# Per-head products in a vision tower: full-height matmuls split into two row halves, in two phases

## What is computed

```
kv = jnp.einsum('bhlk,bhlv->bhkv', k, v)
out = jnp.einsum('bhlk,bhkv->bhlv', q, kv)
```

## Time and profile before

| | us |
|---|---|
| median of 3 runs | 1691.65 (1689.15 to 1692.24) |
| the profiled execution, its own time | 1688.76 |
| its span in the profile | 1686.6 |
| TensorE matmul busy | 1482.2 (88%) |
| TensorE weight loads busy | 1437.1 (85%) |
| VectorE busy | 1020.7 (61%) |
| ScalarE busy | 872.3 (52%) |
| GpSimd busy | 111.1 (7%) |

### The profile page before, as it was taken

One profiled execution on the slowest core, in us unless ns is written; L12 is line 12 of the kernel. 1 busy time (PEld: TensorE's weight loads), 2 busy tenths in 40 slices (PEclk: granted clock), 3 DMA queues, 4 the chain that ended last, 5 costly groups with the idle time before them and its releaser, 6 DMA issues. The chain is left out here.

```text
span 1686.6 us, 32100 instructions
## 1 busy us (share of the span) xinstructions
PE 1482.2 (88%) x9909; PEld 1437.1 (85%) x9909; DVE 1020.7 (61%) x2461; ACT 872.3 (52%) x3121; POOL 111.1 (7%) x240
## 2 busy tenths in 40 slices
PE   5899999999999999999999999999999998563211
PEld 5899999999999999999999999999999997441110
DVE  6765566666665655556555565556665542766676
ACT  4455555555555555555555555555555555541320
POOL 0000000000000000000000000000000000000000
PEclk9999999999999999999999999999999999556555
DMA  9211111111111111111111111111100001374007
GB/s 200 74 44 44 43 42 42 42 42 42 42 42 42 42 42 40 40 40 40 41 42 42 42 42 42 42 42 42 42 10 10 10 10 39 122 268 174 0 0 305
DMA packets 53092, 99.34 MB, mean 59 GB/s; under 512 B 16705, under 2 KB 35649, under 8 KB 52033
## 3 DMA queue, kind: packets, MB, share of 16 engines
q1 hardware_dynamic: 50768, 96.91, 19.7%
q10 hardware_dynamic: 2288, 2.00, 0.6%
HBM read 73.17 MB, written 25.69 MB: 59 GB/s over the span
## 5 line engine op out<-in xcount | busy, mean ns | idle before, releaser
L613 ACT ACTIVATE ffn<-ffn 128x196 f32<-128x196 f32 x1024 | 329.7, 322 | 236.8 <-PE ffn L504 236.3
L504 PE MATMUL ffn<-x_t_hi,pat_w_hi 128*128 128x392 f32 x1024 | 360.6, 352 | 1.7 <-DVE x_t_lo L772 1.7
L504 PE MATMUL ffn<-x_t_hi,pat_w_lo 128*128 128x392 f32 x1024 | 348.6, 340 | 0.0
L504 PE MATMUL ffn<-x_t_lo,pat_w_hi 128*128 128x392 f32 x1024 | 348.2, 340 | 0.0
L435 PE MATMUL gen<-qkvu_w_hi,h_t_hi 128*98 128x256 f32 x768 | 215.4, 280 | 1.4 <-ACT q_t L571 1.4
L435 PE MATMUL gen<-qkvu_w_hi,h_t_lo 128*98 128x256 f32 x768 | 215.0, 280 | 0.0
L435 PE MATMUL gen<-qkvu_w_lo,h_t_hi 128*98 128x256 f32 x768 | 214.7, 280 | 0.0
L504 PEld LDWEIGHTS ffn<-x_t_hi,pat_w_hi 128*128 128x128 f32 x1024 | 193.1, 189 | 2.0 <-DVE x_t_lo L772 2.0
L504 PEld LDWEIGHTS ffn<-x_t_lo,pat_w_hi 128*128 128x128 f32 x1024 | 194.3, 190 | 0.0
L613 ACT ACTIVATION_READ_ACCUMULATOR ffn<-ffn 128x1 f32 x1024 | 194.3, 190 | 0.0
L504 PEld LDWEIGHTS ffn<-x_t_hi,pat_w_lo 128*128 128x128 f32 x1024 | 192.9, 188 | 0.0
(11 more groups left out here) (190 smaller groups left out, 2750.3 us busy)
## 6 DMA issues: line engine op xcount, KB each, us to landing
raw<-in_x_dram SPq DMA_DIRECT2D x752, 56.0 KB, 2.0
h_dram<-h SPq DMA_DIRECT2D x128, 98.0 KB
process_nat<-ocess_input_weights_dram SPq DMA_DIRECT2D x8, 1024.0 KB, 4.8
process_t<-h_dram SPq DMA_DIRECT2D x8, 896.0 KB, 11.2
out_dram<-process_t SPq DMA_DIRECT2D x8, 896.0 KB, 6.7
h_early<-h_dram SPq DMA_DIRECT2D x4, 896.0 KB, 11.9
out_dram<-h_early SPq DMA_DIRECT2D x4, 896.0 KB, 4.0
pat_nat<-_ffn_input_patterns_dram SPq DMA_DIRECT2D x1, 2048.0 KB, 15.7
```

The source lines that it names most:

```text
L504: last = pe.matmul(fb[f % FFN_BANKS][:, 0:T2], a[:, d, f * P:(f + 1) * P], b[:, d, :], start=n == 0, stop=n == 3 * s.halves - 1)
L613: last = act.activation(cols, cols, ACT.Gelu, accum_out=gelu_sum[:, par, at:at + 1])
```

## The change

`heads` is called twice per pair, as `heads0` ahead of f4 and as `heads1` after it. Each of the 8 products of 128 x 128 becomes two of 64 x 64: the upper 64 features of q with the upper left quarter of kv, and the lower 64 with the lower right quarter. The two off-diagonal quarters, which the mask leaves zero, are no longer multiplied. In `heads0` image 0 takes its upper half and image 1 its lower half, alternating; in `heads1` it is the other way round. So neighbouring matmuls read different partition halves and write different banks. `heads0` now waits for both `kv_masked` and `gate_made` first; `heads1` waits for a new semaphore, `heads_half`, which the last two matmuls of `heads0` raise. `heads_done` rises for both images at the end of `heads1`. ScalarE and VectorE do their part of the step at `heads1` only.

```diff
-            "kvu0 kvu1 q f0 kvu2 o0 kvu3 f1 kvu4 o1 kvu5 f2 kv o2 f3 f4 heads tok f5 b0 f6 b1 f7 b2 turn_g "
+            "kvu0 kvu1 q f0 kvu2 o0 kvu3 f1 kvu4 o1 kvu5 f2 kv o2 f3 heads0 f4 heads1 tok f5 b0 f6 b1 f7 b2 turn_g "
...
-            def heads(i, j, _):
-                p = 2 * i + j
-                pe.wait_ge(kv_masked, p + 1)
-                for img in range(PAIR):
-                    if img == 1:
-                        pe.wait_ge(gate_made, 2 * p + 1)
-                    for t in range(2):
-                        for m in range(s.halves):
-                            last = pe.matmul(gb[(2, 0)[img]][0:T, t * D + m * P:t * D + (m + 1) * P],
-                                             q_t[:, m, tok_cols(img, t)], kv[:, img, m, :], start=True, stop=True)
-                    last.then_inc(heads_done, 1)
+            def heads(i, j, n):
+
+                p = 2 * i + j
+                if n == 0:
+                    pe.wait_ge(kv_masked, p + 1)
+                    pe.wait_ge(gate_made, 2 * p + 1)
+                else:
+                    pe.wait_ge(heads_half, 2 * p + 2)
+                done = {}
+                for t in range(2):
+                    for m in range(s.halves):
+                        for img in range(PAIR):
+                            u = img if n == 0 else 1 - img
+                            at = t * D + m * P + u * ROWS
+                            rows = slice(u * ROWS, (u + 1) * ROWS)
+                            done[img] = pe.matmul(gb[(2, 0)[img]][0:T, at:at + ROWS], q_t[rows, m, tok_cols(img, t)],
+                                                  kv[rows, img, m, u * ROWS:(u + 1) * ROWS], start=True, stop=True)
+                if n == 0:
+                    for img in range(PAIR):
+                        done[img].then_inc(heads_half, 1)
+                else:
+                    for img in range(PAIR):
+                        done[img].then_inc(heads_done, 1)
...
-            def squares(i, j, _):
-                p = 2 * i + j
+            def squares(i, j, n):
+                p = 2 * i + j
+                if n == 0:
+                    return
...
-            def norm_and_gate(i, j, _):
-                p = 2 * i + j
-
+            def norm_and_gate(i, j, n):
+                p = 2 * i + j
+                if n == 0:
+                    return
```

More of the change, by code:

```diff
@@ L204, in tower @@
         q_done, kvu_done, kv_done = sem("q_done"), sem("kvu_done"), sem("kv_done")
-        heads_done, g_turned, wo_done = sem("heads_done"), sem("g_turned"), sem("wo_done")
+        heads_half, heads_done, g_turned, wo_done = sem("heads_half"), sem("heads_done"), sem("g_turned"), sem("wo_done")
         x2_turned, ffn_done = sem("x2_turned"), sem("ffn_done")
@@ L226, in patch_part @@
             return part[:, ks].rearrange("p (n w r) -> p n w r", n=PAIR, w=s.cols)
+        ROWS = P // 2
         TOK, TURN_H, X2 = (1, 3), (2, 3), (0, 1)
```

## The result

The changed kernel takes 1701.89 us (median of 4 runs, 1700.07 to 1702.96) against 1691.76 us before: ratio 1.0064, 95% interval 1.0051 to 1.0076. By the medians it is 10.1 us slower, by the ratio 10.8. The forecast was 1699.9. The profiled execution has 1702.96 us and a span of 1701.2.

The account below looks back on a forecast made before the run. TensorE's unbroken matmul stream was taken as the bound: per pair 1.33 + 0.65 - 1.74 = +0.24 us, times 32 +7.7, plus 0.5 in the last pair, +8.2 on 1691.65 = 1699.9 us; range 1674 to 1724.

Parts of the forecast that it names:

- The bound: Tower: TensorE is one unbroken stream of matmuls, busy 1374.40 of 1389.30 us; what a pair adds or removes counts 32 times.
- Pace of the half products: In heads: weight loads of 98 columns set 16 side-by-side steps of 0.083 us, 1.33 us per pair, ends 0.87 and 2.66.
- Rival D: In heads: row halves don't load side by side; +1.57 us per pair, +50 us, or +29 without a drain; chance 0.12.
- The switch: Between full height and halves, four times per pair: 0.163 us each, the array's way out alone, 0.65 us in all.
- Rival A: At the four switches: no drain, so faster by 0.31 us per pair, -10 us, 1682 us; chance 0.32.
- B: At the four switches: about 0.1 us each eats the gain exactly, no change, 1688 to 1695 us; chance 0.12.
- Rival C: At the four switches: drain plus exposed weight load, 1.04 us per pair, +20 us, 1712; counted within the forecast's 0.44.
- Sum: Per pair: 1.33 + 0.65 - 1.74 = +0.24 us, times 32 is +7.7 us; +8.2 us with the last pair.
- Mask: Wait for the mask copy before heads0, one FFN tile earlier: with a draining switch early by 0.27 us, costs nothing.
- `heads_half`: Added wait before heads1: nothing, as six matmuls of f4, 1.07 us, lie between; some 0.2 us once in the first pair.
- `heads_done` for both at the end: Both images finish at heads1's end: over 2 us of slack before g takes it; 0.5 us lost once, last pair.

Follow-up runs that it names:

- experiment 2: Changed kernel with the same 32 instructions of 64 columns, each reading all 128 rows instead of a row half: 1726.77 us, ratio 1.0215 to the kernel before.
- experiment 7: Changed kernel with only 66 of each tile's 98 tokens multiplied, so weight loads have 66 columns (result incomplete): 1689.83 us, ratio 0.9996 to the kernel before.
- experiment 3: Changed kernel with both phases cut in two again, eight switches instead of four in the inner pairs: 1723.04 us, ratio 1.0189 to the kernel before.
- experiment 10: Changed kernel with heads0 directly behind k^T v, so no FFN tile covers the mask copy: 1729.80 us, ratio 1.0233 to the kernel before.
- experiment 6: Changed kernel with f4 moved ahead of heads0, so heads1 follows heads0 directly: 1700.80 us, ratio 1.0063 to the kernel before.
- experiment 1: Changed kernel's two phases kept, products full height again, one image per phase: 1692.38 us, ratio 1.0015 to the kernel before.
- experiment 8: Kernel before with heads untouched, k^T v cut into 64 x 64 column halves and the mask copy in two pieces: 1674.01 us, ratio 0.9899.
- experiment 5: Kernel before with row halves in one block without inner wait, a bank per half, order f3 f4 heads tok: 1695.56 us, ratio 1.0031.
- experiment 4: Changed kernel with images not alternating: per phase 8 instructions of one row half, then 8 of the other: 1727.60 us, ratio 1.0220 to the kernel before.
- experiment 9: Changed kernel with k^T v cut into column halves as well, without clearing kv: 1690.23 us, ratio 0.9999 to the kernel before.

## Why the prediction was right

- **The bound.** TensorE's stream, every step times 32. Held: the inner periods make 10.8 us, the medians 10.1 and the ratio 10.8.
- **Pace of the half products.** Taken as bound by the load, 16 steps of 0.083 = 1.33 us, side by side. Measured 16 x 0.087 = 1.39. Experiments 2 and 7 show that it is the load: alone and at full height it has the same pace, and with 66 columns it is 0.060. Rival D, no overlap, is out: the halves start 7 ns apart. What the prediction quotes from the Trainium skill for it, that a weight load overlaps running matmuls only where the row groups differ, does not hold here as it stands: at full height the load at 831.13 starts with the full-height matmul at 831.12.
- **The switch.** Taken 0.163 us, between 0 and 0.27; measured 0.17 (0.14 in, 0.20 out, and 0.17 from experiment 3). The size was right and the reason only in part. I had taken the whole way out of the array and a load that goes ahead. It is a shorter wait, 0.09 us, and a load that does not go ahead. That the two errors cancel is luck. The Trainium skill (TensorEngine Tiling (Array Packing), Key Properties) states that a change of mode drains the engine; the trace agrees: 0.27 us from the last full-height start to the first half product, with its load starting only 0.07 us before the last old result's recorded end. Rival A, no drain, falls by it, and so does B, which needed 0.10 us per switch. Rival C was right that the load is laid open. Its 1.04 us per pair against 0.69 measured are too high because it adds the whole 0.163 us of the way out, where 0.09 shows, and a whole load going in, where 0.05 shows.
- **Sum.** +0.24 per pair forecast, +0.35 measured: 0.06 from the step of 0.087, 0.04 from the switches (4 x 0.174 instead of 4 x 0.163). With the first and last pair +8.2 us against 10 to 11.
- **Mask.** Priced at nothing as long as a switch covers it; experiment 10 prices the cover at 0.9 us per pair. My estimate of its end, 0.27 us ahead of the need, is 0.2 in the trace.
- **`heads_half`.** Nothing with f4 between; 0.3 us without it (experiment 6), where I had 0.26.
- **`heads_done` for both at the end.** Nothing in the inner pairs (experiment 1: 0.03 us). In the last pair TensorE waits 4.53 us for g where it was 3.87; 0.5 was forecast.

What I had not seen ahead is the version of experiment 8. The rule that made this change lose, load against stream, says where halves win.

## What to carry to other kernels

In this kernel, splitting a block-diagonal product into array halves paid where both the moving columns and the columns of the weight load shrank: k^T v in one visit fell from 1.79 to 1.28 us per pair, and the kernel gained 1.0%. The product q kv, whose load stayed at 98 columns, came out even in one visit (1.73 against 1.74 us, experiment 5) and lost 0.6% in two. Count per visit as well as per matmul: entering and leaving the split layout costs 0.35 us together, so as many halves as possible belong into one visit. They should alternate between the halves in program order; one half after the other, only 8 of 16 overlapped (experiment 4). When a step moves ahead of its cover, check what still hides its producer: here one FFN tile of 1.07 us hid 0.9 us of mask copy.

## What was not expected of the hardware

- A matmul of the other row half starts ahead of its turn, by some four instructions (experiment 4: 8 of 16 overlapped although the program had them one half after the other).
- Row halves and column halves pay the same for a visit, 0.35 us, although the one splits the rows and the other the columns.
- Unchanged code differs between profiles by the clock that TensorE is granted. The 8 matmuls of 512 columns in the routed stage take 1.94 us before and 3.7 us in experiments 5, 6 and 9, whose profiles also have a routed stage 2.5 to 2.8 us longer. Windows of experiment 9 and, the same stretch of the stage, of the kernel before (busy, instructions, granted clock):

```profile
1555.00:1565.00 10.00, 7.03 (x27) 0.50 0.01 2
```

```profile
1557.00:1567.00 10.00, 6.35 (x28) 0.73 0.00 0
```

At 0.50 the engine is at its 1.2 GHz level throughout; before, part of the stretch ran at 2.4. In that stage TensorE stands idle for long stretches, and the level rises later in the longer profiles; what decides it is not shown. It can differ between executions of one kernel: of the five of experiment 6, three at 0.929 and 0.930 took 1700.0 to 1700.8 us, and two at 0.927, the profiled one among them, 1702.5 and 1702.8. So a time can carry 2 to 3 us of this, a quarter of the effect that was to be measured, and the period of the inner pairs is free of it.
